# Attention kernel on one Trainium2 core: weighting runs of two tiles, and a fourth bank for the maxima

## The chip, the cores and the metric

The kernel runs on one core of a Trainium2 chip (trn2). The number reported is the device time of one execution in microseconds (us). The kernel before takes 1761.29 us, the median of three runs (1760.61 to 1761.71).

The core has five instruction queues: TensorE (PE), which multiplies 128-row tiles into the eight banks of PSUM; VectorE (DVE); ScalarE (ACT); GpSimd (POOL); and SyncE (SP), which here only issues DMAs. Each works through its instructions in order, and they wait for each other by counting semaphores.

## The reference

A gated cross-attention layer followed by a gated mixture-of-experts layer; only the first matters here. Four batches, 512 queries each, 16 heads of width 32. The context of 1601 rows is split into 257 image rows and 1344 text rows, and each part has a softmax of its own:

```python
x = x + tanh(g_xattn) * xattn(layernorm(x), ctx_2048, ...)
q = rms_norm(linear(x, q_w, q_b), norm_q_w)            # 16 heads of 32
k, v = rms_norm(linear(ctx_txt, k_w, k_b), ...), linear(ctx_txt, v_w, v_b)
k_img, v_img = ...                                      # the same for the image rows
img_x = attention(q, k_img, v_img)                      # softmax(q k / sqrt(32)) v
txt_x = attention(q, k, v)
out = linear(txt_x + img_x, o_w, o_b)
x = x + tanh(g_ffn) * ffn(layernorm(x), ...)
```

## The kernel before

The program has three stages: projections (to about 400 us of the span), attention (about 400 to 1213 us), experts (the rest). The change is in the attention.

**Groups and steps.** The attention runs over 16 groups G of four heads of one batch. A group has 13 steps kt, one for each tile of 128 keys: tiles 0 to 9 are text, tile 10 is half text and half image, 11 and 12 are image. In one step PE makes four score matmuls, one for each head (`score`, L989, keys by 512 queries), into banks 2 to 4 in turn. ACT takes the exponential of each into a buffer P (L1128). There are four P buffers, used in turn by the tiles. PE then multiplies P by the values: `weigh` (L944), eight instructions for each tile in the trace, all into bank 6 in four column strips of 32, where they accumulate over the tiles of the text. POOL adds up the exponentials of tiles 0 to 7 in SBUF (L1342, 128x2048), in step kt the tile kt-1, in steps 2 to 8. DVE adds half of tile 7, and tiles 8 and 9, in steps 11 and 12. ACT may fill the P buffer of tile kt+4 only when tile kt has been both weighted and added.

**Maxima.** Softmax needs the row maxima of the next group before it begins. While group G is scored, PE also makes 64 "units" of group G+1 (`pe_max_unit`, L446: queries of one head by 448 or 258 keys), and DVE reduces each to its maximum (`dve_max_unit`, L639). `UNITS` gives how many stand in each step: 7, 6, 4, 6, 5, 6, 6, 5, 6, 5, 6, 2, 0. They are numbered here from 0, so that step 3 begins with unit 17. The units use banks 0, 1 and 5 in turn (`BANKS_RA`), so that a unit waits for the reduction of the unit three before it (`ra_bank`). In groups 5, 9 and 15 the steps 4, 6, 8 and 10 also hold twelve matmuls each of the output projection (L49 to L51), which take a bank of the same ring.

**Order within a step on PE.** `scored(0)`, `place(0)`, `scored(1)`, `place(1)`, then the weighting of the step, then `place(2)`, `scored(2)`, `place(3)`, `scored(3)`, `place(4)` to `place(6)`; `place(i)` is a unit. Before, step 3 weights tiles 0 and 1, steps 4 to 10 one tile each (tile kt-2), and step 11 tiles 9 and the text half of 10.

**Bank 7, the totals.** In step 12 of group G and in step 0 of the next, PE sums the text into bank 7 (`both_halves_of_10`, L1017, and `image`, L944 with `sacc`), and ACT copies it out (`txt_total`, L1138). In step 1 PE sums the image into the same bank (`image_total`, 24 instructions at L944 with `ones`). In step 2 DVE does, between its units, three multiplications of 128x512: `oi` (L1261, reads bank 6), `ot` (L1264, reads bank 7) and `rt` (L1267, reads bank 7). The last two raise `d_img`, which stands at 2G once both of group G-1 are done. Bank 7 is then unused until step 12.

Of the kernel before, what the change touches and what calls it, by code (L numbers as in the profile page):

```python
# [13 lines left out]
NB = 4  # L14
# [5 lines left out]
NKT = 13  # L20
# [4 lines left out]
NG = 4 * NB  # L25
# [13 lines left out]
def program(nc, ap, ctx):  # L39
# [71 lines left out]
    p_ra, d_ra = sem("p_ra"), sem("d_ra")  # L111
# [105 lines left out]
    def rows_ra(G):  # L217


        return 64 + 65 * G + 4 * sum(x < G for x in (5, 9))  # L220
# [621 lines left out]
    dnh, dnl = [in_kst0(4096, 2, 512)], [in_kst0(5120, 2, 512)]  # L842
    early = Vg[0][:, 0:8, :].rearrange("p a b -> p (a b)").rearrange("p (k n) -> p k n", k=2)

    BANKS_RA = (0, 1, 5)
    NSTEP = NKT * NG + 2
    LASTG = NKT * (NG - 1)


    UNITS = (7, 6, 4, 6, 5, 6, 6, 5, 6, 5, 6, 2, 0)  # L850
    PLAN = [[1] * n + [0] * (7 - n) for n in UNITS]

    def exp_no(G, kt, j):
        return 52 * G + 4 * kt + j + 1
# [11 lines left out]

    def sum_no(G, kt):
        return 7 * G + max(1, kt)


    PROJECTED = {5: 0, 9: 1, 15: 2}

    def a_high(G):

# [78 lines left out]
    def pe_attend():  # L953
        pe.wait_ge(d_mm, NMM)
        ra = 65

        def ra_bank():
            if ra >= 68:
                pe.wait_ge(d_ra, ra - 2)
            return BANKS_RA[(ra - 65) % 3]  # L960

        def units(G, m, n):
            nonlocal ra
            for i in range(m, m + n):
                s = G % 2
                if i == 0:
                    pe.wait_ge(s_key[s][0], 48 + 96 * (G // 2))
                    pe.wait_ge(s_qry[G % 3], 48 * (G // 3 + 1))
                if i == 14:
                    pe.wait_ge(s_key[s][1], 144 * (G // 2 + 1))  # L970
                pe_max_unit(G, i, ra, ra_bank())
                ra += 1

        def score(G, kt, j):
            s, m = G % 2, 128 if kt < 12 else 65
            e = exp_no(G, kt, j)
            if kt == 0 and j == 0:
                pe.wait_ge(s_key[s][0], 48 + 96 * (G // 2))
                pe.wait_ge(s_qry[G % 3], 48 * (G // 3 + 1))
                pe.wait_ge(s_mrow[s], 32 * (G // 2 + 1))  # L980
                if G == 0:
                    pe.wait_ge(g_ind, 4)
                if G == 1:
                    pe.wait_ge(s_ind1, 16)
            if kt == 10 and j == 0:
                pe.wait_ge(s_key[s][1], 144 * (G // 2 + 1))
            if e > 3:
                pe.wait_ge(a_exp, e - 3)
            pe.matmul(ps[:m, 2 + (e - 1) % 3, :], Kst[s][0:100, j, 128 * kt:128 * kt + m], Qst[G % 3][0:100, j, :],  # L989
                      start=True, stop=True).then_inc(p_sc, 1)  # L990

        def weigh(G, kt, p0, p1_, first, last):
            s = G % 2
            if kt == 0:
                pe.wait_ge(s_val[s], 80 * (G // 2 + 1))
                if G:
                    pe.wait_ge(d_oi, G)
                else:
                    pe.wait_ge(a_tr, NTR)
                    pe.wait_ge(d_tr, NTR)  # L1000
            pe.wait_ge(a_exp, exp_no(G, kt, 3))
            pe_heads(6, lambda j: Vg[s][p0:p1_, kt, 32 * j:32 * j + 32], P[slot(G, kt)], p0, p1_, first, last).then_inc(p_pv, 1)

        def total(G, kt, p0, p1_, first, last):
            pe_heads(7, lambda j: ones[p0:p1_, :], P[slot(G, kt)], p0, p1_, first, last).then_inc(p_tot, 1)

        def text_end(G):
            weigh(G, 9, 0, 128, False, False)
            weigh(G, 10, 0, 64, False, True)

        def both_halves_of_10(G):

            pt = P[slot(G, 10)]
            pe.wait_ge(a_txt, 2 * G + 1)
            pe.wait_ge(d_img, 2 * G) if G else pe.wait_ge(d_ones, 1)
            for j in range(4):
                tot = pe.matmul(ps[32 * j:32 * j + 32, 7, :], ones[0:64, :], pt[0:64, j, :],  # L1017
                                start=True, stop=False, tile_position=(0, 32 * j))
                pv = pe.matmul(ps[32 * j:32 * j + 32, 6, :], Vg[G % 2][64:128, 10, 32 * j:32 * j + 32], pt[64:128, j, :],
                               start=True, stop=False, tile_position=(64, 32 * j))  # L1020
            tot.then_inc(p_tot, 1)
            pv.then_inc(p_pv, 1)

        def image(G):

            weigh(G, 11, 0, 128, False, False)
            weigh(G, 12, 0, 65, False, True)
            pe.wait_ge(d_add, 4 * G + (4 if G < NG - 1 else 9))
            pe_heads(7, lambda j: ones[:, :], sacc, 0, 128, False, True).then_inc(p_tot, 1)

        def image_total(G):
            pe.wait_ge(a_txt, 2 * G + 2)
            total(G, 10, 64, 128, True, False)
            total(G, 11, 0, 128, False, False)
            total(G, 12, 0, 65, False, True)

        for step in range(NSTEP):
            G, kt = divmod(step, NKT)
            more = G + 1 < NG
            plan = PLAN[kt] if more else [0] * 7  # L1040
            at = sum(map(sum, PLAN[:kt])) if more else 0
            upto = [at + sum(plan[:i]) for i in range(8)]

            def place(i):
                units(G + 1, upto[i], plan[i])

            def scored(j):
                if G < NG:
                    score(G, kt, j)

            if kt == 0:
                place(0)
                place(1)
                if G:
                    image(G - 1)
                place(2)
                for j in range(4):
                    scored(j)
                    place(3 + j)
                continue  # L1060
            scored(0)
            place(0)
            scored(1)
            place(1)
            if kt == 1 and G:
                image_total(G - 1)
            if kt == 3:
                weigh(G, 0, 0, 128, True, False)
            if 3 <= kt < 11:
                weigh(G, kt - 2, 0, 128, False, False)  # L1070
            if kt == 11:
                text_end(G)
            if kt == 12:
                both_halves_of_10(G)
                if more:
                    pe.wait_ge(d_mx, G + 2)
                    pe.wait_ge(d_ra, ra)
                    pe_mrow(BANKS_RA[(ra - 65) % 3])
                    ra += 1
            place(2)  # L1080
            scored(2)
            place(3)
            scored(3)
            place(4)
            place(5)
            place(6)
            if G in PROJECTED and kt in (4, 6, 8, 10):
                b = PROJECTED[G]
                if kt == 4:
                    pe.wait_ge(a_ath, 4 * b + 4)  # L1090
                    pe.wait_ge(g_atl, 4 * b + 4)
                    if b == 0:
                        pe.wait_ge(g_wol, 4)
                pe_project_tile(b, (kt - 4) // 2, ra_bank())
                ra += 1
        for t in range(4):
            pe.wait_ge(a_ath, NG + t)
            pe.wait_ge(d_last, 4 * t + 12)
            pe_project_tile(NB - 1, t, ra_bank())
            ra += 1  # L1100
# [7 lines left out]
    def act_attend():  # L1108
# [41 lines left out]
        for step in range(NSTEP):  # L1150
# [5 lines left out]
            for j in range(4):  # L1156
                if G < NG:
                    exps(G, kt, j)
                    if kt == 11 and j == 1:
                        txt_weighed(G)  # L1160
                    if kt == 12 and j == 1 and G + 1 < NG:
                        act_rows_high(G + 1, BANKS_RA[(rows_ra(G + 1) - 65) % 3])
            if step == NKT * NG - 1:
                split(NG - 2)
            if step == 2:
# [40 lines left out]
    def dve_attend():  # L1206
# [4 lines left out]
        def units(G, m, n):  # L1211
            nonlocal ra
            for i in range(m, m + n):
                dve_max_unit(i, ra, BANKS_RA[(ra - 65) % 3])
                ra += 1

        def add_half_of_7(G):
# [21 lines left out]
        for step in range(NSTEP):  # L1239
# [37 lines left out]
            elif kt == 12:  # L1277
                add_to_sum(G, 9, slice(0, 2))
                if more:
                    dve_rows_low(G + 1, BANKS_RA[(ra - 65) % 3])  # L1280
                    ra += 1
                add_to_sum(G, 9, slice(2, 4))
            else:
                units(G + 1, at, sum(plan))
            if G in PROJECTED and kt in (4, 6, 8, 10):
                dve_project_tile(PROJECTED[G], (kt - 4) // 2, ra, BANKS_RA[(ra - 65) % 3])
                ra += 1
            for i in range(3):
                if step == LASTG + 4 + 3 * i:
# [24 lines left out]
        for t in range(4):  # L1314
# [6 lines left out]
            dve.wait_ge(a_ath, NG + t)  # L1321
            dve.tensor_tensor(a_low(NG - 1)[:, cs], oi[:, cs], a_high(NG - 1)[:, cs].bitcast(F32), ALU.subtract).then_inc(d_last, 1)
            if t:
                dve_project_tile(NB - 1, t - 1, ra, BANKS_RA[(ra - 65) % 3])
                ra += 1
        dve_project_tile(NB - 1, 3, ra, BANKS_RA[(ra - 65) % 3])
        variance(NB - 1)
        inverse_root(NB - 1)

# [875 lines left out]
```

## Time and profile before

| | |
|---|---|
| Median of three runs | 1761.29 us (1760.61 to 1761.71) |
| The profiled execution, its own time | 1759.23 us |
| Its span | 1757.9 us |
| PE busy | 1692.5 us, 96% of the span |
| DVE busy | 1212.7 us, 69% |
| POOL busy | 876.6 us, 50% |
| ACT busy | 821.1 us, 47% |
| One plain group of the attention (start of `rt`, L1267, 460.3, 507.9, 555.5 us in groups 1 to 3) | 47.6 us |

The shares are means over stages. The last row is the distance between the same instruction of two groups that follow each other. The rows below are those of one plain group, G = 10 (its step 2 ends at about 916 us), of one group with projection, G = 5 (650 to 700 us), and of places where PE stood still. A row of the timeline gives the start, the time from the start of its first to the end of its last instruction, the engine, the line and tiles, how many instructions it merges, and in brackets how long the engine was idle before it and who released it.

### The profile page before, as it was taken

To read this page: it belongs to the slowest core of one execution; us is meant where nothing else is said; L and a number is where in the kernel's file an instruction comes from. 1 tells how busy PE (TensorE), PEld (TensorE's weight loads), DVE (VectorE), ACT (ScalarE), POOL (GpSimd) and SP (SyncE) were. 2 spreads that over 40 slices of the span, in tenths; PEclk is the share of its full clock that TensorE was granted. 3 is DMA by queue.
4 is the path that set the end of the run, shared out by engine and by line. 5 is a ranking of instruction groups with operands and counts; after the bars stand their busy time and mean duration, and the time that the engine had idled before them with its cause. 6 is when DMAs were issued, how large, how long until landed. Compare 5 with 4: busy or idle time off the path is not lost. (4 is left out here: it accounts for less than half of the span.)

```text
span 1757.9 us, 24703 instructions
## 1 busy us (share of the span) xinstructions
PE 1692.5 (96%) x8694; PEld 1111.2 (63%) x8694; DVE 1212.7 (69%) x2246; ACT 821.1 (47%) x1519; POOL 876.6 (50%) x316
## 2 busy tenths in 40 slices
PE   5999999999999999999999999997999999999999
PEld 4888878885444445444444444444777778878777
DVE  5776677667888887888878888875545454443565
ACT  4443322336666664666556666661321355554221
POOL 3121312116766664777736667710514466766542
PEclk9999999999999999999999999998999999999999
DMA  9456858646455552555445544221312488876433
GB/s 314 138 178 187 248 174 205 184 162 194 129 149 149 143 135 53 139 147 148 127 121 147 125 113 129 78 83 41 126 43 102 141 276 260 272 261 227 154 116 96
DMA packets 198603, 273.04 MB, mean 155 GB/s; under 512 B 30968, under 2 KB 128008, under 8 KB 197964
## 3 DMA queue, kind: packets, MB, share of 16 engines
q1 hardware_dynamic: 193360, 254.67, 49.2%
q0 software_dynamic: 5120, 16.78, 2.8%
q8 instruction: 70, 1.15, 0.3%
q14 instruction: 53, 0.43, 0.1%
HBM read 198.15 MB, written 106.18 MB: 173 GB/s over the span
## 5 line engine op out<-in xcount | busy, mean ns | idle before, releaser
L1128 ACT ACTIVATE P<-ps 128x512 f32<-128x512 f32 (+1 forms) x832 | 444.1, 596 | 261.4 <-PE ps L989 213.7
L639 DVE TENSOR_REDUCE mp<-ps 128x1 f32<-128x448 f32 x768 | 430.0, 615 | 87.1 <-PE ps L446 86.7
L446 PE MATMUL ps<-Kst,Qst 96*128 96x448 f32 (+1 forms) x1024 | 383.3, 389 | 5.8 <-DVE mp L639 5.5
L1342 POOL TENSOR_TENSOR sacc<-sacc,P 128x2048 f32<-128x2048 f32 x90 | 379.8, 4220 | 12.9
L989 PE MATMUL ps<-Qst,Kst 100*128 100x512 f32 (+1 forms) x832 | 322.2, 408 | 9.1 <-ACT P L1128 8.8
L446 PEld LDWEIGHTS ps<-Kst,Qst 96*128 96x128 f32 x1024 | 192.4, 188 | 213.5 <-DVE mp L639 142.2
L944 PE MATMUL ps<-P,Vg 128*32 128x512 f32 (+2 forms) x1664 | 216.0, 603 | 0.4 <-ACT P L1128 0.3
L815 POOL TENSOR_TENSOR cl<-craw,ch 128x1024 fp32r<-128x1024 f32 (+2 forms) x26 | 62.0, 2386 | 285.6 <-ACT ch L551 285.6
L989 PEld LDWEIGHTS ps<-Qst,Kst 100*128 100x128 f32 (+1 forms) x832 | 152.0, 185 | 69.0 <-ACT P L1128 43.2
L49 PE MATMUL ps<-W,ch 128*128 128x512 f32 (+1 forms) x408 | 162.5, 398 | 0.0
L51 PE MATMUL ps<-W,cl 128*128 128x512 f32 (+1 forms) x408 | 159.7, 391 | 0.0
L50 PE MATMUL ps<-W,ch 128*128 128x512 f32 (+1 forms) x408 | 159.4, 391 | 0.0
L2104 POOL TENSOR_TENSOR gul<-gur,guh 128x2048 fp32r<-128x2048 f32 x15 | 69.4, 4626 | 118.4 <-ACT guh L1777 118.4
L639 DVE TENSOR_REDUCE mx<-ps 128x1 f32<-128x258 f32 x256 | 96.2, 421 | 31.7 <-PE ps L446 31.1
L1342 POOL TENSOR_TENSOR sacc<-P 128x2048 f32<-128x2048 f32 x15 | 68.8, 4586 | 69.0 <-ACT P L1128 43.8
L1350 POOL TENSOR_TENSOR oi<-oi,ot 128x512 f32<-128x512 f32 x15 | 19.1, 1277 | 154.4 <-DVE sacc L1237 136.8
L2104 POOL TENSOR_TENSOR Kst<-gur,Kst 128x2048 fp32r<-128x2048 f32 x15 | 69.4, 4626 | 45.2 <-ACT Kst L1777 45.2
L51 PEld LDWEIGHTS ps<-W,cl 128*128 128x128 f32 (+1 forms) x408 | 75.8, 186 | 17.8 <-issue 0.2
L49 PEld LDWEIGHTS ps<-W,ch 128*128 128x128 f32 (+1 forms) x408 | 76.0, 186 | 15.4
L50 PEld LDWEIGHTS ps<-W,ch 128*128 128x128 f32 (+1 forms) x408 | 76.0, 186 | 15.3
L571 ACT ACTIVATE junk<-kf 128x512 f32<-128x512 f32 (+1 forms) x51 | 32.1, 630 | 107.7 <-DVE kf L687 107.7
L944 PEld LDWEIGHTS ps<-P,Vg 128*32 128x32 f32 (+2 forms) x1664 | 34.3, 107 | 72.4 <-ACT P L1128 45.8
(241 smaller groups left out, 3087.7 us busy)
## 6 DMA issues: line engine op xcount, KB each, us to landing
gur<-in_w_gate_up SPq DMA_DIRECT2D x23, 1024.0 KB
Kst<-KHd SPq DMA_DIRECT2D x56, 320.0 KB, 4.8
Vd<-vf SPq DMA_DIRECT2D x50, 256.0 KB, 2.3
craw<-in_ctxT SPq DMA_DIRECT2D x24, 512.0 KB, 4.5
KHd<-sth SPq DMA_DIRECT2D x24, 512.0 KB, 3.5
KLd<-stl SPq DMA_DIRECT2D x24, 512.0 KB, 4.7
dnr<-in_w_down SPq DMA_DIRECT2D x23, 512.0 KB, 3.9
xg<-Xg SPq DMA_DIRECT2D x23, 512.0 KB, 7.9
```

The lines of the kernel that those rows point to most:

```text
L49: pe.matmul(out, ah, bh, start=first, stop=False)
L50: pe.matmul(out, ah, bl, start=False, stop=False)
L51: return pe.matmul(out, al, bh, start=False, stop=last)
L446: pe.matmul(ps[:, bank, 0:c1 - c0], Qst[G % 3][0:96, j, 128 * qt:128 * qt + 128], Kst[G % 2][0:96, j, c0:c1], start=True, stop=True).then_ ...
L571: act.activation(junk[:rows], kf[:rows, u % 3, :], ACT.Square, accum_out=stk[:rows, u % 4, 0:1]).then_inc(a_sqk, 1)
L639: dve.reduce_max(out, ps[:, bank, 0:c1 - c0], AX.X).then_inc(d_ra, 1)
L815: pool.tensor_tensor(cl[:, n % 3, :, 0:c1 - c0], craw[:, n % 3, :, 0:c1 - c0], ch[:, n % 2, :, 0:c1 - c0].bitcast(F32), ALU.subtract).then ...
L944: ins = pe.matmul(ps[32 * j:32 * j + 32, bank, :], w(j), pt[p0:p1_, j, :], start=first, stop=last, tile_position=(p0, 32 * j))
L989: pe.matmul(ps[:m, 2 + (e - 1) % 3, :], Kst[s][0:100, j, 128 * kt:128 * kt + m], Qst[G % 3][0:100, j, :], start=True, stop=True).then_inc( ...
L1128: act.activation(P[slot(G, kt)][:m, j, :], ps[:m, 2 + (e - 1) % 3, :], ACT.Exp, scale=SCALE).then_inc(a_exp, 1)
L1342: pool.tensor_tensor(sacc[:, h], (P[slot(G, 0)] if kt == 1 else sacc)[:, h], P[slot(G, kt)][:, h], ALU.add).then_inc(g_sum, 1)
L2104: pool.tensor_tensor(gul[q % 2], gur[raw_slot(q)][:], guh[q % 2].bitcast(F32), ALU.subtract).then_inc(g_gu, 1)
```

## The change

Two things are changed, both in the attention.

First, the weighting. Tiles 2 to 7 are weighted two to a run, in steps 5, 7 and 9 (tiles kt-3 and kt-2), as tiles 0 and 1 already are in step 3. Steps 4, 6 and 8 weight nothing, and step 10 weights tile 8.

Second, the ring of the maxima. In steps 3 to 9 (of groups that have a next one) the units and projection tiles take whichever of banks 0, 1, 5 and 7 was used longest ago; in the other steps, of banks 0, 1 and 5. `banks_of_maxima` works the list out, and each filling waits for the reduction of the last one in its bank. Since bank 7 holds the totals up to step 2, PE waits in step 3, behind `scored(0)` and ahead of `place(0)`, for `d_img` at 2G; and in step 12, ahead of the totals, for the last unit in bank 7.

```diff
+    def banks_of_maxima():
+        fills, last = [], {0: None, 1: None, 5: None, 7: None}
+        for step in range(NSTEP):
+            G, kt = divmod(step, NKT)
+            n = (UNITS[kt] + (kt == 12)) * (G + 1 < NG) + (G in PROJECTED and kt in (4, 6, 8, 10)) + 4 * (step == NSTEP - 1)
+            for _ in range(n):
+                free = (0, 1, 5, 7) if 3 <= kt < 10 and G + 1 < NG else (0, 1, 5)
+                b = min(free, key=lambda i: -1 if last[i] is None else last[i])
+                fills.append((b, last[b]))
+                last[b] = 65 + len(fills) - 1
+        return fills
...
         def ra_bank():
-            if ra >= 68:
-                pe.wait_ge(d_ra, ra - 2)
-            return BANKS_RA[(ra - 65) % 3]
+            bank, last = FILLS[ra - 65]
+            if last is not None:
+                pe.wait_ge(d_ra, last + 1)
+            return bank
...
             pe.wait_ge(d_img, 2 * G) if G else pe.wait_ge(d_ones, 1)
+            if G + 1 < NG:
+                pe.wait_ge(d_ra, last_in_bank_7(G) + 1)
...
             scored(0)
+            if kt == 3 and G and more:
+                pe.wait_ge(d_img, 2 * G)
             place(0)
             scored(1)
             place(1)
             if kt == 1 and G:
                 image_total(G - 1)
-            if kt == 3:
-                weigh(G, 0, 0, 128, True, False)
-            if 3 <= kt < 11:
+            if kt in (3, 5, 7, 9):
+                weigh(G, kt - 3, 0, 128, kt == 3, False)
                 weigh(G, kt - 2, 0, 128, False, False)
+            if kt == 10:
+                weigh(G, 8, 0, 128, False, False)
```

How the instructions stand on PE from the end of step 2 to the two weightings of step 3, in group 1. L446 is a unit, the `Qst,Kst` rows are scores, the 32x512 rows are the weighting. Before:

```order
L446 MATMUL ps<-Kst,Qst 128x448 [waits d_ra]
L989 MATMUL ps<-Qst,Kst 128x512 [waits a_exp] x2
L446 MATMUL ps<-Kst,Qst 128x448 [waits d_ra]
L989 MATMUL ps<-Qst,Kst 128x512 [waits a_exp]
L446 MATMUL ps<-Kst,Qst 128x448 [waits d_ra]
L944 MATMUL ps<-P,Vg 32x512 [waits a_exp,d_oi,s_val1]
```

After, the same place:

```order
L446 MATMUL ps<-Kst,Qst 128x448 [waits d_ra]
L1012 MATMUL ps<-Qst,Kst 128x512 [waits a_exp] x2
L446 MATMUL ps<-Kst,Qst 128x448 [waits d_ra,d_img]
L1012 MATMUL ps<-Qst,Kst 128x512 [waits a_exp]
L446 MATMUL ps<-Kst,Qst 128x448 [waits d_ra]
L966 MATMUL ps<-P,Vg 32x512 [waits a_exp,d_oi,s_val1]
```

Nothing moved here, but the first unit of step 3 now waits for `d_img` as well, and the second score, the second unit and the weighting stand behind it. The second place is step 4 and the beginning of step 5 of the same group. Before:

```order
L989 MATMUL ps<-Qst,Kst 128x512 [waits a_exp]
L446 MATMUL ps<-Kst,Qst 128x448 [waits d_ra]
L989 MATMUL ps<-Qst,Kst 128x512 [waits a_exp]
L446 MATMUL ps<-Kst,Qst 128x448 [waits d_ra]
L944 MATMUL ps<-P,Vg 32x512 [waits a_exp]
L944 MATMUL ps<-P,Vg 32x512 x3
L446 MATMUL ps<-Kst,Qst 128x448 [waits d_ra]
L989 MATMUL ps<-Qst,Kst 128x512 [waits a_exp]
```

After:

```order
L1012 MATMUL ps<-Qst,Kst 128x512 [waits a_exp]
L446 MATMUL ps<-Kst,Qst 128x448 [waits d_ra]
L1012 MATMUL ps<-Qst,Kst 128x512 [waits a_exp]
L446 MATMUL ps<-Kst,Qst 128x448 [waits d_ra]
L1012 MATMUL ps<-Qst,Kst 128x512 [waits a_exp]
L446 MATMUL ps<-Kst,Qst 128x448 [waits d_ra]
L1012 MATMUL ps<-Qst,Kst 128x512 [waits a_exp]
```

The weighting that stood in the middle of step 4 is gone from there, so that units and scores alternate until the middle of step 5, where two tiles are weighted behind one another.

## Rows read from the trace of the kernel before

**Rows 1.** The page: span, and busy time, share and instructions of each engine.

```profile
span 1757.9 us, 24703 instructions
...
PE 1692.5 (96%) x8694; PEld 1111.2 (63%) x8694; DVE 1212.7 (69%) x2246; ACT 821.1 (47%) x1519; POOL 876.6 (50%) x316
```

**Rows 2.** Timeline of PE, group 10, end of step 2 to step 4.

```profile
913.00 0.63 PE L989 MATMUL ps<-Qst,Kst 100*128 100x512 f32 x2
913.47 0.37 PE L446 MATMUL ps<-Kst,Qst 96*128 96x448 f32 x1
...
914.35 0.47 PE L446 MATMUL ps<-Kst,Qst 96*128 96x448 f32 x1 [0.28 <-DVE mp L639]
914.74 1.92 PE L944 MATMUL ps<-P,Vg 128*32 128x512 f32 x16
916.60 0.47 PE L446 MATMUL ps<-Kst,Qst 96*128 96x448 f32 x1
916.91 0.39 PE L989 MATMUL ps<-Qst,Kst 100*128 100x512 f32 x1
```

**Rows 3.** Timeline of DVE, group 10, steps 1 to 5.

```profile
909.88 3.28 DVE L639 TENSOR_REDUCE mp<-ps 128x1 f32<-128x448 f32 x6 [2.22 <-PE ps L446]
...
915.34 0.68 DVE L1267 TENSOR_TENSOR rt<-rt,ps 128x512 f32<-128x512 f32 x1
915.93 4.45 DVE L639 TENSOR_REDUCE mp<-ps 128x1 f32<-128x448 f32 x8
920.75 2.75 DVE L639 TENSOR_REDUCE mp<-ps 128x1 f32<-128x448 f32 x5 [0.37 <-PE ps L446]
923.89 2.22 DVE L639 TENSOR_REDUCE mp<-ps 128x1 f32<-128x448 f32 x4 [0.39 <-PE ps L446]
```

**Rows 4.** Timeline of PE, group 10, around the weightings of steps 5 and 9 to 11.

```profile
922.10 0.36 PE L446 MATMUL ps<-Kst,Qst 96*128 96x448 f32 x1
922.39 1.07 PE L944 MATMUL ps<-P,Vg 128*32 128x512 f32 x8
923.38 0.47 PE L446 MATMUL ps<-Kst,Qst 96*128 96x448 f32 x1
923.70 0.40 PE L989 MATMUL ps<-Qst,Kst 100*128 100x512 f32 x1
923.93 0.37 PE L446 MATMUL ps<-Kst,Qst 96*128 96x448 f32 x1
...
937.09 0.39 PE L446 MATMUL ps<-Kst,Qst 96*128 96x258 f32 x1
...
941.89 2.06 PE L944 MATMUL ps<-P,Vg 128*32 128x512 f32 x16
```

**Rows 5.** Timeline of POOL and of ACT, group 10: the adds, and who waits for them.

```profile
911.28 4.59 POOL L1342 TENSOR_TENSOR sacc<-P 128x2048 f32<-128x2048 f32 x1 [3.09 <-ACT P L1128]
916.01 26.02 POOL L1342 TENSOR_TENSOR sacc<-sacc,P 128x2048 f32<-128x2048 f32 x6
939.58 2.12 ACT L1128 ACTIVATE P<-ps 128x512 f32<-128x512 f32 x4 [0.74 <-POOL sacc L1342]
942.11 1.08 ACT L1128 ACTIVATE P<-ps 128x512 f32<-128x512 f32 x2 [0.41 <-POOL sacc L1342]
```

**Rows 6.** Timeline of PE and DVE, group 5, behind the first projection tile.

```profile
659.55 0.40 PE L989 MATMUL ps<-Qst,Kst 100*128 100x512 f32 x1
659.75 0.75 DVE L1189 SCALAR_TENSOR_TENSOR acc<-ps,tg,acc 128x512 f32<-128x512 f32 x1 [2.12 <-PE ps L51]
```

**Rows 7.** Windows around pauses of PE: busy times, clock, DMA share, GB/s.

```profile
29.00:32.00 3.00, 3.00 (x8) 2.32 (x8) 1.62 (x5) 1.18 (x5) 0.00 (x0) 0.50 1.07 369
37.00:39.00 2.00, 2.00 (x9) 1.64 (x10) 2.00 (x2) 0.00 (x0) 1.40 (x1) 1.00 1.06 384
1200.00:1203.00 3.00, 3.00 (x9) 2.33 (x8) 0.22 (x1) 0.00 (x0) 0.00 (x0) 0.50 0.00 0
```

**Rows 8.** Timeline of PE: the first matmul behind a pause.

```profile
28.79 0.57 PE L49 MATMUL ps<-Kst,Qst 128*128 128x512 f32 x1 [1.97 <-DVE Qst L625]
...
36.91 0.48 PE L49 MATMUL ps<-Kst,Qst 128*128 128x512 f32 x1 [2.66 <-DVE Qst L625]
...
1197.28 0.77 PE L49 MATMUL ps<-Woh,Qst 128*128 128x512 f32 x1 [3.87 <-ACT Qst L1182]
```

More of the change, by code:

```diff
@@ L843, in program @@
     early = Vg[0][:, 0:8, :].rearrange("p a b -> p (a b)").rearrange("p (k n) -> p k n", k=2)
-    BANKS_RA = (0, 1, 5)
     NSTEP = NKT * NG + 2
@@ L851, in program, with bank_of, last_in_bank_7 @@
     PLAN = [[1] * n + [0] * (7 - n) for n in UNITS]
+    PROJECTED = {5: 0, 9: 1, 15: 2}
+    def banks_of_maxima():
[9 more added lines that the diff above has]
+        return fills
+    FILLS = banks_of_maxima()
+    def bank_of(ra):
+        return FILLS[ra - 65][0]
+    def last_in_bank_7(G):
+        return max(65 + i for i, (b, _) in enumerate(FILLS[:rows_ra(G + 1) - 65]) if b == 7)
     def exp_no(G, kt, j):
@@ L868, in sum_no @@
         return 7 * G + max(1, kt)
-    PROJECTED = {5: 0, 9: 1, 15: 2}
     def a_high(G):
@@ L1077, in pe_attend @@
                     pe.wait_ge(d_ra, ra)
-                    pe_mrow(BANKS_RA[(ra - 65) % 3])
+                    pe_mrow(bank_of(ra))
                     ra += 1
@@ L1161, in act_attend @@
                     if kt == 12 and j == 1 and G + 1 < NG:
-                        act_rows_high(G + 1, BANKS_RA[(rows_ra(G + 1) - 65) % 3])
+                        act_rows_high(G + 1, bank_of(rows_ra(G + 1)))
             if step == NKT * NG - 1:
@@ L1213, in units @@
             for i in range(m, m + n):
-                dve_max_unit(i, ra, BANKS_RA[(ra - 65) % 3])
+                dve_max_unit(i, ra, bank_of(ra))
                 ra += 1
@@ L1279, in dve_attend @@
                 if more:
-                    dve_rows_low(G + 1, BANKS_RA[(ra - 65) % 3])
+                    dve_rows_low(G + 1, bank_of(ra))
                     ra += 1
@@ L1285, in dve_attend @@
             if G in PROJECTED and kt in (4, 6, 8, 10):
-                dve_project_tile(PROJECTED[G], (kt - 4) // 2, ra, BANKS_RA[(ra - 65) % 3])
+                dve_project_tile(PROJECTED[G], (kt - 4) // 2, ra, bank_of(ra))
                 ra += 1
@@ L1323, in dve_attend @@
             if t:
-                dve_project_tile(NB - 1, t - 1, ra, BANKS_RA[(ra - 65) % 3])
+                dve_project_tile(NB - 1, t - 1, ra, bank_of(ra))
                 ra += 1
-        dve_project_tile(NB - 1, 3, ra, BANKS_RA[(ra - 65) % 3])
+        dve_project_tile(NB - 1, 3, ra, bank_of(ra))
         variance(NB - 1)
```

## The prediction

> **What bounds the kernel now.** I read the shares of the engines first, then one plain group of the attention on PE, DVE, POOL and ACT in the timeline, then a group with projection, then the places where PE paused. PE is busy 96% of the span [rows 1]. In the attention this is not the whole truth: in steps 3 to 8 PE is paced by DVE. At each run of weighting DVE runs out of filled banks, 0.37 and 0.39 us of idleness [rows 3], and afterwards PE waits for banks to be reduced, as in the wait of 0.28 us ahead of unit 18 [rows 2]. From step 9 on, where units are short, PE goes at its own pace. A third chain runs beside both: POOL adds seven tiles without a pause from 911.28 to 942.03 us [rows 5], and ACT, which may refill a P buffer only after the add, waits for it in steps 10 and 11 (0.74 and 0.41 us). PE's own arrival at the text end of step 11, 941.89 us [rows 4], lies only some 0.3 us behind what this chain would allow: the first exponential of step 10 can't start before 939.58, the second and third follow at 0.52 us each, so the second score of step 11, which waits for the bank of the third, can't start before about 941.2, and a weighting 0.3 to 0.4 behind it at 941.6. So a plain group could gain at most 0.3 us even if PE got much faster, while what PE loses beyond nothing is lost in full, since steps 11 to 1 are a chain through PE, ACT and back.
>
> **What the merging of runs gives.** A run of one tile takes 0.99 us to the next unit (922.39 to 923.38), a run of two 1.86 (914.74 to 916.60) [rows 2, 4]: 0.12 saved. Entering a run costs 0.29 from the unit ahead instead of the usual 0.21, leaving it 0.32 (923.38 to 923.70) instead of 0.21 [rows 4]: 0.19 more. A merge is worth 0.31 us of PE, three in a group, 48 in all: 15 us if PE were the bound everywhere. Where DVE is the bound they are worth what DVE's idleness loses. That is easily counted. A single run leaves DVE idle 0.38 us. A run of two is 0.87 us longer, and the fourth bank holds one reduction more, 0.55 us (3.28 us for six) [rows 3]: idle 0.38 + 0.87 - 0.55 = 0.70 us for a pair, against 0.76 for the two single runs. In steps 3 to 7 the change gives DVE nothing.
>
> **What the new wait costs.** In step 3 the first unit now waits for both multiplications that read bank 7. Unit 17 started at 913.47 [rows 2]. The last multiplication starts at 915.34 and takes 0.68 [rows 3], so it ends at 916.02. It can't come sooner: from 909.88 DVE works without a pause, eight reductions and three multiplications. With 0.06 us for the release (unit 15's reduction ended 914.29, unit 18 started 914.35) unit 17 starts at 916.08, 2.61 us later. Behind it on PE stand the second score, unit 18 and the run of tiles 0 and 1, in this order. Before, PE ran this pair of tiles just while DVE worked off its backlog; now it runs them when DVE has only units 17 and 18 to do. Step by step: score at 916.39, unit 18 at 916.62, run at 916.91 (0.29 behind), unit 19 at 918.77 (1.86 on), against 916.60 before: 2.17 us later. DVE gets unit 19 at 919.28 (0.51 behind it, as 909.37 to 909.88 did), against 915.93 + 2 x 0.556 = 917.04: 2.24 us later.
>
> **Does it come back?** From here DVE is the bound. To the end of step 7 it had four idle stretches before, 0.37, 0.39 and two like them, 1.4 us together. After, step 4 has no run and no idleness, the pairs of steps 5 and 7 leave 0.70 each: 1.4 us. The lag stays 2.2 us. In steps 8 and 9 the last merge is worth up to 0.31 on PE, less a little of renewed waiting for banks ahead of the pair, where four units are to be reduced. I take 2.0 us late at the first unit behind the pair of step 9 (before: 937.09 [rows 4]), and the same at step 11: 2.0 us for the group. The ends: at best PE has none of the waits for DVE it had (the 25.3 us from 916.60 to 941.89 hold about 23.9 us of work by its own spacings: 29 long units at 0.21, 16 short at 0.125, 32 scores at 0.235, seven runs at 0.99 + 0.19 with both halves of the transition), so 1.4 of waits go and 0.9 of merges come: 2.2 - 1.4 - 0.9 = -0.1, and the floor of the POOL chain is -0.3. At worst the whole stall stays and nothing is gained: +2.6. Between them I keep 2.0, since rows 3 show DVE, not PE, as what repeats the pace.
>
> In the groups with projection (5 and 9) PE is slower than DVE: DVE stands 2.12 us idle ahead of the first projection tile's evacuation [rows 6], so the lag of 2.2 shrinks there to about 1.1 at the end of step 4 (twelve matmuls finish at 659.55 before, by my count at 660.6 after), and the merges then give 0.2 or so in all: I take 0.9 for the group; ends -0.9 and 2.2. Group 0 has no wait in step 3 and is held by POOL in step 10: nothing. Group 15 has no units; its pairs let ACT's queue of three score banks run dry for a moment, 1.86 us of run against 3 x 0.52 of exponentials, 0.3 lost, 0.31 won each: nothing, bounds +-1 us. The waits in step 12 for the last unit in bank 7 are long met, since DVE has reduced all units by step 11. No DMA is moved; the load of keys in step 5 waits for scores that come 2 us later, with most of two groups to spare.
>
> **The sum.** Of groups 1 to 14, twelve are plain: 12 x 2.0 = 24.0. Two with projection: 1.8. The rest 0. The profiled execution took 1759.23 us (span 1757.9), which gives 1785.0; on the median of 1761.29, 2.1 above it, the forecast is 1787.1 us. I say 1787.
>
> **Rivals.**
>
> (a) PE makes it good. If the fourth bank lets PE run ahead so that its work, not DVE's, sets the pace from step 4, the 1.4 us of waits and the 0.9 of merges cover the stall: -0.1 us a group, -0.3 at the floor that POOL sets, so 1757 to 1760 us. For it: DVE is busy only 69% of the span [rows 1]. Against: in these steps it is idle just 0.4 us in some 3.5. It decides, on no change and then on faster, from the point where 2.2 us come back in steps 4 to 10. The Trainium skill (TensorEngine Tiling (Array Packing), Key Properties) says that changing the tiling mode drains TensorE, which would make every removed transition a gain; the 0.19 us of rows 4 agree that a transition costs something, and by that rule alone the sum would be 48 x 0.31 = 15 us faster, 1746 us.
>
> (b) Half is made good. DVE's stretches are a little shorter than I count, or the pace of the units after the stall is PE's in step 4: 0.3 to 1.4 us lost in a plain group, 1766 to 1779 us. For it: DVE is given nothing to do from 917.8 to 919.3, so PE has free banks for a while.
>
> (c) The clock falls. PE stands still for about 2.5 us in each of 14 groups. Behind a pause of 3.87 us the granted clock was 0.50, that is 1.2 GHz (1200 to 1203 us), behind one of 1.97 us too (29 to 32), but not behind one of 2.66 us (37 to 39 at 1.00, 2.4 GHz) [rows 7, 8]. At the lower level eight matmuls from 28.79 on took 3.4 us where at the higher they take 1.9: 1.5 us lost each time, up to 14 x 1.5 = 21 on top of the forecast, 1808 us. Before the pause PE is dense here, as it was before the 2.66 us one. The Trainium skill (TensorE: Matmul & The Clock Gate, HAM oscillation) says that waits repeated in every iteration can make the matmuls behind each of them run at the half rate; it would give the 1808 of this rival, and the trace of before has pauses of this length with either outcome.
>
> (d) The drain is not there: `d_img` comes before PE gets to step 3. The rows exclude it for a plain group (915.34 against 913.47), so this is worth little.
>
> **Chances.** Forecast 0.62 (1779 to 1797), (b) 0.14, (c) in full or in most groups 0.09, (a) 0.09, and 0.06 for no change of more than 0.2%, where lag and gains happen to cancel. 0.2% is 3.5 us, about what a measurement of this kernel can tell from none. The range 1770 to 1801 takes in the forecast, two thirds of (b) and the beginning of (c). Faster 0.07, same 0.07, slower 0.86.
>
> **What would show it.** In the profile after: in each of groups 1 to 14 the first unit of step 3 with an idle PE of about 2.4 us ahead of it, released by the DVE instruction that writes `rt`; right behind the run of tiles 0 and 1 DVE idle some 1.5 us, and about 0.7 at the runs of steps 5 and 7; the distance of plain groups 49.6 us instead of 47.6; ACT waiting no longer for POOL in steps 10 and 11, since PE comes later than the adds. Runs of two tiles at 1.86 us would confirm the saving. The forecast is wrong if the distance stays at 47.6 although the stall is there (then DVE had more to give than the rows show), or if the clock row of the attention is below 1.00.

## The result, and the profile after

The changed kernel takes 1811.82 us, the median of four runs (1807.27 to 1815.65), against 1760.99 us before (1760.61 to 1761.71): 1.0288 times as long, 95% interval 1.0264 to 1.0312. I had forecast 1787 us, range 1770 to 1801. The direction was right, the size was not: 51 us lost instead of 26. The profiled execution took 1811.14 us.

The page of the changed kernel, to be read against [rows 1], and the row that says who made PE wait ahead of its units:

```profile
span 1809.8 us, 24717 instructions
...
PE 1710.1 (94%) x8694; PEld 1123.3 (62%) x8694; DVE 1211.8 (67%) x2246; ACT 820.7 (45%) x1519; POOL 875.1 (48%) x316
...
L446 PE MATMUL ps<-Kst,Qst 96*128 96x448 f32 (+1 forms) x1024 | 378.4, 390 | 36.7 <-DVE rt L1295 34.2
```

PE's units now stand behind 34.2 us of idleness that ends with DVE's `rt` instruction: 14 groups, 2.44 us each. PE's busy time grew too, by 17.6 us, although it does the same 8694 matmuls; the sum of the forecast has no term for this. The timeline of PE in two groups shows both. Group 11 first, which was the only one of the fourteen whose clock stayed up, then group 12; this answers to [rows 2]:

```profile
1002.07 0.47 PE L446 MATMUL ps<-Kst,Qst 96*128 96x448 f32 x1 [2.45 <-DVE rt L1295]
1002.38 0.39 PE L1012 MATMUL ps<-Qst,Kst 100*128 100x512 f32 x1
1002.61 0.36 PE L446 MATMUL ps<-Kst,Qst 96*128 96x448 f32 x1
1002.90 1.92 PE L966 MATMUL ps<-P,Vg 128*32 128x512 f32 x16
1004.75 0.47 PE L446 MATMUL ps<-Kst,Qst 96*128 96x448 f32 x1
...
1051.32 0.47 PE L446 MATMUL ps<-Kst,Qst 96*128 96x448 f32 x1 [2.44 <-DVE rt L1295]
...
1052.50 3.19 PE L966 MATMUL ps<-P,Vg 128*32 128x512 f32 x16
1055.62 0.47 PE L446 MATMUL ps<-Kst,Qst 96*128 96x448 f32 x1
```

The run of tiles 0 and 1 takes 1.85 us to the next unit in group 11 (1002.90 to 1004.75), as before, and 3.12 in group 12 (1052.50 to 1055.62). The windows over both (busy time and count of PE, PEld, DVE, ACT and POOL, then the granted clock, DMA share, GB/s):

```profile
1001.40:1005.00 3.60, 2.93 (x20) 1.15 (x21) 1.77 (x4) 0.60 (x1) 3.46 (x2) 1.00 0.68 294
...
1050.00:1055.00 5.00, 3.68 (x15) 1.17 (x19) 2.51 (x5) 0.60 (x1) 4.86 (x2) 0.67 0.50 215
```

And DVE in group 11, which answers to [rows 3]:

```profile
1001.34 0.68 DVE L1295 TENSOR_TENSOR rt<-rt,ps 128x512 f32<-128x512 f32 x1
1002.58 1.16 DVE L639 TENSOR_REDUCE mp<-ps 128x1 f32<-128x448 f32 x2 [0.56 <-PE ps L446]
1005.26 5.93 DVE L639 TENSOR_REDUCE mp<-ps 128x1 f32<-128x448 f32 x11 [1.53 <-PE ps L446]
1011.89 2.22 DVE L639 TENSOR_REDUCE mp<-ps 128x1 f32<-128x448 f32 x4 [0.69 <-PE ps L446]
...
1019.15 2.22 DVE L639 TENSOR_REDUCE mp<-ps 128x1 f32<-128x448 f32 x4 [0.69 <-PE ps L446]
...
1025.24 1.97 DVE L639 TENSOR_REDUCE mx<-ps 128x1 f32<-128x258 f32 x5 [1.15 <-PE ps L446]
...
1050.59 0.68 DVE L1295 TENSOR_TENSOR rt<-rt,ps 128x512 f32<-128x512 f32 x1
```

DVE stands idle 0.56 and 1.53 us behind its last multiplication, then 0.69 at each pair. From one `rt` to the next, 1001.34 to 1050.59, is 49.25 us, where it was 47.57 before. Of the other plain groups most take 50.8 to 50.9, and groups 8 and 10 take 51.8 and 51.9. In these two, and in group 5, the clock is at the lower level for about 7 us, in the others for about 3.6. ACT waits for POOL hardly any more, 3.2 us in the whole execution (it was 0.74 and 0.41 in one group alone [rows 5]):

```profile
L1156 ACT ACTIVATE P<-ps 128x512 f32<-128x512 f32 (+1 forms) x832 | 443.2, 598 | 302.9 <-PE ps L1012 267.5 <-issue 25.1 <-POOL sacc L1370 3.2
```

Of the 51.9 us between the two profiled executions, 47.0 lie between `rt` of group 1 and `rt` of group 15, where the wait is. Group 0 has 1.4 of the rest; 1.7 lie ahead of it (in the first 50 us the clock is 0.93 here and was 0.97), and 1.8 behind `rt` of group 15. No run explains these last two.

### The profile page after: what moved, and what is told of

Its sections match the earlier page's. It is cut to its first block and busy times, and to the rows that moved or that the text cites. A ratio compares the mean times of both kernels' runs of the same rounds, so it can differ in the third digit from the quotient of the medians.

```text
span 1809.8 us, 24717 instructions
## 1 busy us (share of the span) xinstructions
PE 1710.1 (94%) x8694; PEld 1123.3 (62%) x8694; DVE 1211.8 (67%) x2246; ACT 820.7 (45%) x1519; POOL 875.1 (48%) x316
## 5 line engine op out<-in xcount | busy, mean ns | idle before, releaser
L446 PE MATMUL ps<-Kst,Qst 96*128 96x448 f32 (+1 forms) x1024 | 378.4, 390 | 36.7 <-DVE rt L1295 34.2
L446 PEld LDWEIGHTS ps<-Kst,Qst 96*128 96x128 f32 x1024 | 195.2, 191 | 221.8 <-DVE mp L639 99.4
L966 PE MATMUL ps<-P,Vg 128*32 128x512 f32 (+2 forms) x1664 | 226.1, 653 | 0.4 <-ACT P L1156 0.3
L966 PEld LDWEIGHTS ps<-P,Vg 128*32 128x32 f32 (+2 forms) x1664 | 41.5, 113 | 102.4 <-ACT P L1156 57.5
```

Of the source, the lines that this page charges most:

```text
L446: pe.matmul(ps[:, bank, 0:c1 - c0], Qst[G % 3][0:96, j, 128 * qt:128 * qt + 128], Kst[G % 2][0:96, j, c0:c1], start=True, stop=True).then_ ...
L966: ins = pe.matmul(ps[32 * j:32 * j + 32, bank, :], w(j), pt[p0:p1_, j, :], start=first, stop=last, tile_position=(p0, 32 * j))
```

## The experiments

The ratios are against the kernel before on the same chip. The kernel before took 1757.6 to 1758.0 us as a median there, 1754.6 to 1762.6 in single runs, so a few tenths of a per cent are told from rows better than from totals. I compare the distance from one `rt` to the next. All numbers in this table are worked out from the starts of these rows. The column "group 1 to 15" goes from `rt` of group 1 to `rt` of group 15. It has 11 plain groups in it, two with projection (5 and 9), and group 14, whose distance is shorter (42.1 us before), since group 15 places no units. The column "plain group" is of the 11. The rows are of one execution of each kernel, the ratios of four to twelve.

| kernel | plain group | projection group | group 1 to 15 | ratio (95% interval) |
|---|---|---|---|---|
| before | 47.57 | 61.04 | 687.35 | 1 |
| changed | 49.25 (1 of 11), 50.8 to 51.9 | 65.5, 63.7 | 734.38 | 1.0288 (1.0264 to 1.0312) |
| e1, PE kept busy | 49.29 | 62.3 | 710.77 | 1.0159 (1.0130 to 1.0188) |
| e2, bank 7 from step 4 | 47.32 | 60.0 | 682.80 | 0.9997 (0.9987 to 1.0007) |
| e3, pairs only | 48.63 | 61.4 | 701.07 | 1.0103 (1.0081 to 1.0126) |
| e4, bank only | 50.1 or 51.1 | 63.8 | 730.22 | 1.0248 (1.0223 to 1.0273) |
| e5, as e2, group 0 kept | 47.33 | 60.1 | 682.96 | 0.9986 (0.9977 to 0.9995) |
| e6, bank from step 4, no pairs | 47.33 | 59.9, 59.0 | 681.64 | 0.9988 (0.9978 to 0.9999) |
| e7, before, lighter adds | 47.54 | 61.1 | 689.72 | 1.0001 (0.9991 to 1.0010) |
| e8, as e2, lighter adds | 47.09 | 60.1 | 681.95 | 0.9975 (0.9957 to 0.9992) |
| e9, weighting ahead of the wait | 47.59 | 60.6 | 686.85 | 1.0024 (1.0012 to 1.0036) |
| e10, the wait only | 51.3 | 64.8 | 739.71 | 1.0310 (1.0293 to 1.0328) |

**e1, the pause filled.** It tells the clock from the wait.

```diff
             if kt == 3 and G and more:
+                pe.wait_ge(d_oi, G)
+                for _ in range(10):
+                    pe.matmul(ps[:, 6, :], Kst[G % 2][0:100, 0, 0:128], Qst[G % 3][0:100, 0, :], start=True, stop=True)
                 pe.wait_ge(d_img, 2 * G)
```

> The changed kernel, but PE makes ten useless matmuls of 512 columns into bank 6 (0.215 us each, their result is overwritten) ahead of the wait for d_img in step 3 of groups 1 to 14, so that PE does not stand still for 2.45 us; what waits and what follows is the same. Theory A (the time above the forecast is the clock: 13 of 14 groups lose some 1.6 us at 1.2 GHz behind the pause): the granted clock of the attention back at 1.00, every plain group 49.25 us like the one undisturbed group, in all 1811.8 - 21 = 1790 us. Theory B (the wait itself costs more than I counted and the low clock is a side show): the time stays within 5 us of 1811.8.

Measured: 1785.64 us, below the 1790 of theory A and far from theory B. Timeline of PE in step 3 of group 2, then windows over the same group:

```profile
509.14 2.61 PE L1090 MATMUL ps<-Qst,Kst 100*128 100x512 f32 x10 [0.19 <-DVE oi L1292]
511.59 0.37 PE L446 MATMUL ps<-Kst,Qst 96*128 96x448 f32 x1
...
512.33 1.93 PE L966 MATMUL ps<-P,Vg 128*32 128x512 f32 x16
514.18 0.47 PE L446 MATMUL ps<-Kst,Qst 96*128 96x448 f32 x1
...
508.00:516.00 8.00, 7.81 (x41) 4.89 (x41) 5.81 (x11) 3.29 (x6) 7.77 (x2) 1.00 0.83 310
```

The first unit still comes only behind `rt`, but the run behind it takes 1.85 us and the clock is 1.00. All plain groups are at 49.3 us. So between groups 1 and 15, 710.77 - 687.35 = 23.4 us are what the changed kernel loses at full clock, and 734.38 - 710.77 = 23.6 are the price of the clock. The 23.4 are the wait's price less what pairs and bank win; e2 shows that gain without the wait, 4.6 us. Useless work made the kernel 1.3% faster.

**e2, bank 7 from step 4.** The wait stands where it is already met.

```diff
-                free = (0, 1, 5, 7) if 3 <= kt < 10 and G + 1 < NG else (0, 1, 5)
+                free = (0, 1, 5, 7) if 4 <= kt < 10 and G + 1 < NG else (0, 1, 5)
...
-            if kt == 3 and G and more:
+            if kt == 4 and G and more:
```

> The changed kernel with bank 7 in the ring only in steps 4 to 9, the wait for d_img standing in step 4, where the multiplications that read bank 7 are over. Theory A (the wait in step 3 is the whole loss, the pairs of tiles cost nothing): no pause of PE, clock 1.00, DVE idle about 0.7 us at the runs of steps 5 and 7, a plain group 47.3 to 47.6 us with ACT still waiting for POOL in steps 10 and 11; in all 1757 us (1755 to 1762). Theory C (runs of two tiles starve DVE and are the loss): 1780 us or more.

Measured: 1757.73 us, no difference. The plain groups are as expected, 47.32, with ACT waiting for POOL in the last steps (0.57, 1.16 and 0.45 us in group 2), and DVE idle 0.69 and 0.70 at the pairs. 4.6 us are won from group 1 to 15. In the profiled execution they went again in group 0. There PE waits for ACT in step 10, as it did before for 0.84 us, but now 1.29 us, since it comes earlier. Timeline of PE and two windows of it:

```profile
440.17 0.50 PE L1012 MATMUL ps<-Qst,Kst 100*128 100x512 f32 x1 [1.29 <-ACT P L1156]
...
442.09 3.80 PE L966 MATMUL ps<-P,Vg 128*32 128x512 f32 x16
...
443.00:445.00 2.00, 2.00 (x16) 0.20 (x8) 1.87 (x2) 0.12 (x1) 0.00 (x0) 0.50 0.00 0
...
449.00:451.00 2.00, 2.00 (x21) 0.79 (x6) 0.00 (x0) 0.09 (x1) 0.00 (x0) 0.50 0.00 0
```

The clock stood at 0.50, 1.2 GHz, for some ten us, and the stretch from the first score of group 0 to `rt` of group 1 took 63.9 us (402.8 to 466.7) instead of 59.8 (400.5 to 460.3). This is one execution of ten, and the slowest (1761.40 us); that the others lost the same there is not shown.

**e3, pairs without the bank.** The ring is 0, 1, 5 throughout and the wait for `d_img` is gone; the weighting is that of the changed kernel.

> Only the runs of two tiles; the ring keeps banks 0, 1 and 5 and there is no wait for d_img. Theory A: no pause, clock 1.00; but without the fourth bank a run of two leaves DVE idle 0.38 + 0.87 = 1.25 us against 0.76 for two single runs, so 1.0 us lost in steps 5 and 7 and 0.3 won in step 9: +0.7 us in a group, 1771 us in all (1764 to 1776). Theory C: 1780 us or more. If the bank did nothing at all: the same as with the bank from step 4.

Measured: 1775.62 us, plain groups +1.06 us where I expected +0.7. DVE in group 2:

```profile
509.25 7.10 DVE L639 TENSOR_REDUCE mp<-ps 128x1 f32<-128x448 f32 x13
517.58 2.22 DVE L639 TENSOR_REDUCE mp<-ps 128x1 f32<-128x448 f32 x4 [1.23 <-PE ps L446]
```

The 1.23 us at a pair are the 1.25 expected. With the bank it is 0.69: the fourth bank is worth 0.55 us at each pair, one reduction, as reckoned. The two pairs lose 2 x (1.23 - 0.76) = 0.94 us by this; that +1.06 came and not +0.7 suggests that the merge in step 9 gave nothing here.

**e4, the bank without the pairs.** The weighting is that of the kernel before; ring and wait are those of the changed one.

> Only the fourth bank from step 3, with the wait for d_img there; tiles weighted one to a run as before. Theory A: the pause of 2.45 us and the low clock behind it are there, 1.6 us in most groups; the fourth bank covers the 0.38 us of each single run, 1.4 us back of the lag of 2.2: 0.8 us a group and the clock, 14 x 2.4 = 34 at most, 1790 us (1783 to 1797). Theory C: with single runs close to before, 1765 us or less.

Measured: 1801.47 us, 11 above what I named and 4 above the range. The wait and the clock are there without any pair; theory C (pairs are the loss) falls. Timeline of PE in group 2:

```profile
513.08 0.74 PE L446 MATMUL ps<-Kst,Qst 96*128 96x448 f32 x1 [2.44 <-DVE rt L1294]
...
514.55 3.64 PE L966 MATMUL ps<-P,Vg 128*32 128x512 f32 x16
518.12 0.57 PE L446 MATMUL ps<-Kst,Qst 96*128 96x448 f32 x1
```

Here the clock is low from the first matmul behind the pause, and the run takes 3.57 us to the next unit. All fourteen groups are disturbed, so the lag of this kernel at full clock can't be read. The five plain groups at 50.1 and the six at 51.1 differ in how long the clock is low, about 3.6 us in the first and 7 in the others. The pairs are not free beside the wait either: without them groups 1 to 15 take 4.2 us less than in the changed kernel (730.22 against 734.38). How much of this is clock can't be told here.

**e5, group 0 kept as before.** As e2, but with single runs and three banks in group 0.

> The version with bank 7 from step 4, but group 0 as before (one tile to a run, three banks). Theory A says that the pairs and the fourth bank win 0.27 us in a plain group and 1.0 in a group with projection, 4.6 us from group 1 to 15, and that in the version with bank 7 from step 4 this was lost again in group 0, where PE waited 1.29 us for ACT in step 10 and the clock stood at 1.2 GHz from 441 to 451 us (4.1 us lost). Then this kernel takes 4 to 5 us less than the one before, 0.9975 of it. If the loss of group 0 is chance, it stays at 1.000.

Measured: 1756.23 us, 0.9986 of before. PE's wait in step 10 of group 0 is 0.76 us here and the clock stays up; the 59.8 us of group 0 are back (401.8 to 461.6). The rows show 4.4 us won between groups 1 and 15. The ratio lies between the two values named; it stands for 2.5 us, and the medians (1756.23 and 1757.63) differ by 1.4. Where the rest went is not shown; in this profile 1.2 us are lost ahead of group 0, where the clock is 0.93 in the first 50 us and was 0.97. The kernel beats the one before, by little; against e2 (0.9997) its interval overlaps, and the profile of e2 is its slowest execution, so that group 0 ate the gain of e2 is possible and not shown.

**e6, bank from step 4, single runs.**

> Bank 7 in the ring from step 4, tiles weighted one to a run as before. Theory A: the fourth bank takes DVE's idleness at single runs away, so PE would reach step 11 up to 1.4 us earlier, but POOL's chain of adds allows only 0.3: plain groups at 47.3 us just as with pairs; so the pairs are worth nothing beyond it, except 0.6 us in each group with projection. Total within 3 us of before. A rival (the pairs bring the 0.27 us, the bank nothing) has plain groups at 47.6.

Measured: 1754.35 us, plain groups 47.33 as with pairs. In this kernel PE waits for ACT in step 10, which waits for POOL; so what holds the plain group is the same, and the pairs add nothing. I expected them to win 0.6 us in a projection group; they lose 0.2 and 1.0 there. In the first of the two, group 5, this kernel lost some time to the clock:

```profile
690.87 0.45 PE L1012 MATMUL ps<-Qst,Kst 100*65 100x512 f32 x1 [0.85 <-ACT P L1155]
...
692.00:693.00 1.00, 1.00 (x16) 0.00 (x0) 0.90 (x2) 0.30 (x1) 0.00 (x0) 0.50 0.00 0
```

So the 1.0 us of group 9 is the cleaner figure. The bank, not the merging, is what helps.

**e7 and e8, lighter adds.** POOL's adds of tiles 2 to 6 leave out the fourth head; everything else is the kernel before (e7) or e2 (e8).

```diff
-            h = slice(0, 2 if kt == 7 else 4)
+            h = slice(0, 2 if kt == 7 else 4 if kt == 1 else 3)
```

> The kernel before, but POOL leaves out the fourth head in its adds of tiles 2 to 6, so that each takes about a quarter less time (its sums are not complete). Theory A (POOL's chain is nearly, but not quite, the bound before): plain groups 47.5 us, at most 0.1 less than 47.57, since PE has its own work to do; ACT no longer waits for POOL. Rival (POOL is already the bound before): a plain group loses several times that, 1 us or more.

> Pairs and bank 7 from step 4, with the same lighter adds on POOL (the fourth head left out in tiles 2 to 6). Theory A (POOL's chain holds the gain at 0.27 us): without it the three merges of 0.31 us and what the fourth bank adds come through, plain groups 46.5 us (46.3 to 46.9) and 14 us less than before in all, 1744. Rival (DVE is what holds it, 0.7 us idle at each pair): plain groups stay at 47.2 to 47.3.

Measured: 1757.64 and 1754.47 us. In e7 POOL's last six adds take 20.5 us instead of 26.0 and a plain group takes 47.54 instead of 47.57: POOL was not the bound before. (Its 689.7 us in the table are due to the last interval, 44.6 instead of 42.1, where the clock stood at 0.50 from 1148 to 1161 us. e8 has the same there, 43.9 instead of the 41.9 of e2.) In e8 it takes 47.09 instead of 47.32: POOL held 0.23 us, not the 0.8 that theory A gave it, and the whole is 10 us above the 1744 named. DVE in group 2 of e8:

```profile
514.24 2.22 DVE L639 TENSOR_REDUCE mp<-ps 128x1 f32<-128x448 f32 x4 [0.69 <-PE ps L446]
...
521.51 2.22 DVE L639 TENSOR_REDUCE mp<-ps 128x1 f32<-128x448 f32 x4 [0.70 <-PE ps L446]
```

The idleness at the pairs of steps 5 and 7 is unchanged. Neither candidate came true as named: a plain group is 0.5 us under before, of which POOL had hidden half. That DVE's pace hides the rest of the three merges (3 x 0.31 us) fits this idleness, and no run tests it.

**e9, the weighting ahead of the wait.** In step 3 PE does the second score and tiles 0 and 1 first, then waits for `d_img`, then places both units; bank 7 from step 3.

```diff
+            if kt == 3 and G and more:
+                scored(1)
+                weigh(G, 0, 0, 128, True, False)
+                weigh(G, 1, 0, 128, False, False)
+                pe.wait_ge(d_img, 2 * G)
+                place(0)
+                place(1)
...
-            if kt in (3, 5, 7, 9):
+            if kt in (3, 5, 7, 9) and not (kt == 3 and G and more):
```

> The changed kernel with bank 7 from step 3, but in step 3 PE does the second score and the weighting of tiles 0 and 1 ahead of the wait for d_img, and both units behind it. Theory A (what costs is not the wait of the bank but what stands behind it on PE): PE pauses about 0.5 us instead of 2.45, the clock stays at 1.00, unit 19 comes no later than before; plain groups 47.3 us as with bank 7 from step 4, group 0 loses its 1 to 4 us as there, in all 1757 us (1753 to 1761). Theory B (bank 7 can't be had in step 3 at less than about 1.7 us, since DVE stands empty behind the last multiplication in either order): 49 us a group, 1780.

Measured: 1762.25 us. Timeline of PE and DVE in step 3 of group 2:

```profile
508.42 0.87 PE L446 MATMUL ps<-Kst,Qst 96*128 96x448 f32 x3 [0.17 <-DVE rt L1301]
...
507.69 0.67 DVE L1301 TENSOR_TENSOR rt<-rt,ps 128x512 f32<-128x512 f32 x1
508.93 7.00 DVE L639 TENSOR_REDUCE mp<-ps 128x1 f32<-128x448 f32 x13 [0.56 <-PE ps L446]
```

The same wait, with the same matmuls in another order, costs PE 0.17 us instead of 2.44, and a plain group is back at 47.59. It is not at the 47.3 expected; DVE still stands empty 0.56 us behind `rt`, which e2 does not have, and I put the difference down to this. Between groups 1 and 15 it takes 23.9 us less than e1, which has the same bank and pairs and the other order, both at full clock; so in the rows all of the loss was in what stood behind the wait. The totals are less kind: 1762.25 us is 1 above the range, and 0.24% (0.12 to 0.36) slower than before, some 4 us. The profiled execution, 1758.63 us, has none of this. The slower of the ten have a lower mean clock (0.990 and 0.991 at 1763 to 1766 us) than the faster (0.993 and 0.994 at 1758 to 1760), so at least part of it is likely clock; in which step is not shown.

**e10, the wait alone.** The kernel before plus `pe.wait_ge(d_img, 2 * G)` ahead of the first unit of step 3.

> The kernel before with nothing but the wait for d_img ahead of the first unit of step 3: three banks, one tile to a run. Theory A: the lag of 2.2 us is not made good, since DVE loses 0.38 us at each run as before, 2.0 us a group, and the clock 1.6 us in most: plain groups 49.6 us where it holds and 51.2 where it falls, in all about 48 us more than before, 1806. Rival (half of the loss of the changed kernel came from the pairs or the bank): 1785 or less.

Measured: 1811.70 us, 6 above what I named, the plain groups at 51.2 to 51.4 us (expected 51.2 where the clock falls):

```profile
513.90 0.47 PE L446 MATMUL ps<-Kst,Qst 96*128 96x448 f32 x1 [2.44 <-DVE rt L1292]
...
514.84 3.46 PE L966 MATMUL ps<-P,Vg 128*32 128x512 f32 x16
518.23 0.47 PE L446 MATMUL ps<-Kst,Qst 96*128 96x448 f32 x1
```

A kernel that has nothing of the change but its wait takes as long as the changed kernel (1.0310 and 1.0288 of before, intervals that overlap). Between groups 1 and 15 it takes 5.3 us more, about the 4.6 that pairs and bank win without the wait. With e2, which has all but the wait in step 3 and loses nothing, that settles the cause.

## Why the prediction missed

**The bound before: right, with the possible gain a little too high.** I had PE paced by DVE in steps 3 to 8, and POOL's chain close behind. In e2, e5 and e6 a plain group gained 0.25 us before POOL held it (forecast 0.3), and e7 shows that POOL did not bind before.

**The wait: right.** PE was to stand idle about 2.4 us; measured 2.44 to 2.46. DVE was to be idle about 1.5 us behind the run of tiles 0 and 1; measured 1.53. It was to be idle 0.70 at the pairs; measured 0.69.

**Whether it comes back: right in kind, sized 0.3 us too high.** I took 2.0 us lost in a plain group and 0.9 in one with projection. At full clock it was 1.7 (group 11 of the changed kernel, 49.25; all of e1) and 1.3. The lag was there in full at unit 19: in group 11 DVE takes it 3.92 us behind the start of `rt`, against the 1.70 that I reckoned for before, 2.22 us later (forecast 2.24). At the five short units that DVE reduces behind the run of step 9 it was 1.72: 23.90 us behind the start of `rt` in group 11, 22.18 in group 10 before:

```profile
937.52 1.98 DVE L639 TENSOR_REDUCE mx<-ps 128x1 f32<-128x258 f32 x5 [0.79 <-PE ps L446]
```

Half a microsecond came back on the way, where I had allowed 0.2. The sum of these steps, 25.8 us, was measured as 23.4 between groups 1 and 15 in e1.

**The clock: this is the step that failed.** The sum has no term for it: PE's work behind each pause was priced at full speed. I had the fall of the clock only as rival (c), priced at 1.5 us a group and up to 1808 us in all, with a chance of 0.09. The price was nearly right: 1.6 us in most plain groups, up to 3.2 (group 5, 65.5 against the 62.3 of e1), 23.6 in all where I had 21. The chance was not. I let one pause of 2.66 us in the trace of before, behind which the clock stayed up, outweigh those of 1.97 and 3.87, behind which it was down [rows 7, 8]. Rows with opposite outcomes don't exclude an outcome. In the changed kernel 13 of 14 pauses of 2.44 us were followed by 1.2 GHz, in e4 and e10 all 14. The Trainium skill (TensorE: Matmul & The Clock Gate, HAM oscillation) describes such a case: a wait in every iteration, there for a DMA, with the matmuls behind it at half the clock each time. The trace agrees in kind, though the waits of that example are longer than these: the run that takes 1.85 us at full clock takes 2.9 to 3.6 in the 13 groups. I had cited it and then given it a tenth. My own last sign of being wrong, the clock row of the attention below 1.00, is the one that came true.

**The groups that were to cost nothing: group 0 cost 1.4 us.** From the first score to `rt` of group 1 it took 61.2 us (402.3 to 463.4) against 59.8. PE, faster there, waits 1.29 us for ACT in step 10 instead of 0.84, and the clock fell behind it (0.79 from 438 to 446 us). The forecast put this group at nothing, since POOL holds it in step 10.

**The other rivals.** Nothing like the 1.4 us of waits of rival (a) came back, nor a loss as small as that of (b): at full clock 1.7 us stayed. Runs of two do save PE what I said, 1.86 us against 2 x 0.99, but e6 shows that even without the wait they are worth nothing in a plain group; so the 15 us of removed transitions are not there either. The stall that (d) doubted was there in all 14 groups.

## What to carry to other kernels

What this wait cost was decided by what stood behind it on its queue: between groups 1 and 15, at full clock, the kernel with the run of weighting behind the wait took 24 us more than the one with the run ahead of it (e1 and e9). When a wait makes TensorE stand still in every iteration, for some 2.4 us as here, count the clock with it as likely, not as a mishap, and price both. And before you give up a bank or a buffer, or take it at the price of a wait, see in which step it comes free: one step later it was free of charge here.

## What the runs showed of the hardware

Behind the pauses of 2.44 us in step 3 the granted clock fell in 13 of 14 groups of the changed kernel and in all 14 of e4 and e10 (0.50 to 0.70 over the five us from 1 us behind the start of `rt`). It was low for about 3.6 us each time, or for about 7 us: in 3 of the 13 groups of the changed kernel, in 9 of e4, in none of e10. Where the fall comes moves from group to group: in groups 5, 8 and 10 of the changed kernel and in most of e4 while PE still stands still, elsewhere with the first unit or behind it. Group 10 of the changed kernel, a window in the pause and PE's first unit behind it:

```profile
949.00:950.00 1.00, 0.00 (x0) 0.00 (x0) 1.00 (x3) 0.00 (x0) 0.98 (x1) 0.64 0.00 0
...
950.20 0.74 PE L446 MATMUL ps<-Kst,Qst 96*128 96x448 f32 x1 [2.44 <-DVE rt L1295]
```

In e1 ten useless matmuls in the pause kept the clock at 1.00 in every group.

Shorter pauses have either outcome. In group 0 of e2 the clock fell to 0.50 (1.2 GHz) behind a pause of 1.29 us and stayed there for ten us; behind one of 1.29 in the same place of the changed kernel it fell for a shorter time, and behind 1.26 in e1, 1.25 in e9 and 1.45 in e4 not at all. In e6 it fell behind pauses of 1.07 us (group 0) and 0.85 us (group 5). And in e7 and e8 it stood at 0.50 for ten us and more behind group 14, with no pause above 0.4 us in the nine us before:

```profile
1126.00:1135.00 9.00, 7.94 (x57) 2.52 (x61) 4.32 (x4) 5.93 (x13) 2.55 (x2) 1.00 0.46 151
...
1136.00:1145.00 9.00, 9.00 (x36) 3.13 (x36) 5.02 (x5) 5.21 (x10) 0.70 (x1) 0.50 0.34 133
```

These two windows are of e8. So the length of the last pause does not decide it alone; what does was not tried.
